# Two buffers for each block of parts, and a latents stage written out

## The reference

```python
xn = _layernorm(x)                               # mean and variance of a token's 256 numbers
q  = (xn @ Wqa @ Wqb).reshape(b, s, 16, 16)      # by way of 64 numbers a token
kv = (xn @ Wkva @ Wkvb).reshape(b, s, 4, 16, 2)  # by way of 32
k, v = kv[..., 0], kv[..., 1]
q, k = _rope(q), _rope(k)                        # pairs of numbers, turned by cos and sin of the position
logits = xn @ Wg                                 # the experts' router, 8 numbers a token
```

## Time and profile before

| | |
|---|---|
| median of 3 runs | 2279.63 us (2269.03 to 2282.21) |
| the profiled execution | 2277.82 us |
| its span, first to last instruction | 2275.8 us |
| TensorE busy | 2041.2 us, 90% |
| VectorE busy | 1575.5 us, 69% |
| ScalarE busy | 984.8 us, 43% |
| POOL busy | 514.2 us, 23% |
| mean granted TensorE clock over the span | 0.918 |

### The profile page before, as it was taken

The page is one execution under the profiler, slowest core; times in us unless marked ns, Lnnn a source line. Parts: engine busy times, 40 slices in busy tenths (PEclk is TensorE's granted clock), DMA queues, the critical chain, the costliest instruction groups (busy, mean ns, idle before and its releaser), DMA issues. The chain is left out here.

```text
span 2275.8 us, 36321 instructions
## 1 busy us (share of the span) xinstructions
PE 2041.2 (90%) x11618; PEld 1224.9 (54%) x11650; DVE 1575.5 (69%) x3508; ACT 984.8 (43%) x2128; POOL 514.2 (23%) x944
## 2 busy tenths in 40 slices
PE   7869999999999999999499999957728999999998
PEld 3322333333333333332399999945515777777777
DVE  5659998888888888882333333327737899999993
ACT  2222667777777677778344544411111111111112
POOL 2450123322222222222233333346500000000000
PEclk9656999999999999999799999976658999999998
DMA  4445001111111111100522232125430000000005
GB/s 137 141 166 188 27 22 65 58 46 42 43 42 43 41 43 44 41 12 11 158 84 89 89 103 95 52 65 154 146 119 22 19 19 19 19 19 10 10 10 162
DMA packets 124881, 152.22 MB, mean 67 GB/s; under 512 B 12952, under 2 KB 111904, under 8 KB 123808
## 3 DMA queue, kind: packets, MB, share of 16 engines
q1 hardware_dynamic: 85584, 99.48, 13.5%
q10 hardware_dynamic: 31440, 29.62, 3.9%
q0 software_dynamic: 7680, 20.98, 2.9%
HBM read 89.29 MB, written 60.29 MB: 66 GB/s over the span
## 5 line engine op out<-in xcount | busy, mean ns | idle before, releaser
L703 ACT ACTIVATE at_wt<-at_B 128x512 f32<-128x512 f32 (+3 forms) x1280 | 606.1, 538 | 251.1 <-PE at_B L753 244.3
L954 DVE TENSOR_REDUCE at_piece_max<-at_A 128x1 f32<-128x512 f32 x768 | 487.3, 683 | 52.7 <-PE at_A L734 50.8
L771 PE MATMUL at_O<-at_wt,at_v 128*32 128x512 f32 (+3 forms) x2560 | 312.3, 540 | 0.0
L657 POOL TENSOR_SCALAR_AFFINE_SELECT at_wt<-at_wt 128x128 f32<-128x128 f32 x512 | 148.0, 294 | 667.1 <-ACT at_wt L703 658.5
L734 PE MATMUL at_A<-at_k,at_q 96*128 96x512 bf16 (+3 forms) x800 | 275.3, 353 | 8.5 <-DVE at_piece_max L951 2.4
L951 DVE CUSTOM_DVE_ANT_0 at_junk<-at_A,at_hide 128x128 bf16<-128x128 f32 (+3 forms) x512 | 230.7, 487 | 73.0 <-PE at_A L734 69.1
L753 PE MATMUL at_B<-at_q,at_k 99*128 99x512 bf16 (+3 forms) x800 | 273.1, 349 | 5.2 <-ACT at_wt L703 5.2
L1392 PE MATMUL ex_H<-ex_xT,ex_w_in 128*128 128x256 f32 x1920 | 247.7, 285 | 3.2 <-DVE ex_xT L1499 3.2
L1392 PEld LDWEIGHTS ex_H<-ex_xT,ex_w_in 128*128 128x128 f32 x1920 | 236.8, 193 | 3.6 <-DVE ex_w_out L1504 3.6
L1513 DVE TENSOR_TENSOR ex_h<-ex_act_a,ex_H 128x256 f32<-128x256 f32 x160 | 67.2, 420 | 226.8 <-ACT ex_act_a L1441 226.7
L734 PE MATMUL at_A<-s_k,s_q 96*128 96x512 bf16 (+2 forms) x480 | 175.8, 384 | 21.5 <-PEq L93 10.6
(11 more groups left out here) (251 smaller groups left out, 2739.0 us busy)
## 6 DMA issues: line engine op xcount, KB each, us to landing
buf<-s_down ACTq DMA_DIRECT2D x10, 1024.0 KB, 11.0
ex_x<-buf SPq DMA_DIRECT2D x40, 256.0 KB, 2.7
expert_out<-ex_y ACTq DMA_DIRECT2D x40, 256.0 KB, 2.1
ex_raw_in<-in_W_in SPq DMA_DIRECT2D x8, 1024.0 KB, 5.0
q_parts<-parts SPq DMA_DIRECT2D x16, 384.0 KB, 4.8
x<-in_x SPq DMA_DIRECT2D x8, 512.0 KB, 4.5
xn<-xn SPq DMA_DIRECT2D x8, 512.0 KB, 5.3
at_v<-v SPq DMA_DIRECT2D x16, 256.0 KB, 3.5
```

Source lines behind the costliest of these rows:

```text
L657: pool.affine_select(block_, block_, [[1, P]], ALU.is_ge, 0.0, base=0, channel_multiplier=-1).then_inc(hidden, 1)
L703: act.activation(wt[(HP * p + h) % NE_][:, q0:CH], pB_of(p, h, u)[:, q0:CH], ACT.Exp, scale=D ** -0.5).then_inc(wt_ready, 1)
L771: pe.matmul(pO[j % 2][rows, q0:CH], vs[n % 3][:, kt // TPC, kt % TPC, :], wt[(HP * p + h) % NE_][:, q0:CH], start=kt < 2 and not late, sto ...
L954: ins = dve.tensor_reduce(top, pA[slot % NA][:, 0:w], AX.X, ALU.max)
```

## The change

Only `latents` is changed. It does four things.

```diff
-        x = [sb(f"x{u}", [P, TPC, E]) for u in range(2)]
+        x = [s["down"][:, u * TPC:(u + 1) * TPC] for u in range(2)]
...
-        parts = [sb(f"parts{k}", [P, PARTS, CH], BF16) for k in range(3)]
+        parts = [[sb(f"parts{k}{u}", [P, PARTS, CH], BF16) for u in range(2)] for k in range(3)]
...
-        def rounds(eng, chunk):
-
-            with eng.Fori(0, ROUNDS - 2) as j:
-                for u in range(2):
-                    chunk(2 * j + u, u, 4)
-            for c in range(NCH - 4, NCH):
-                chunk(c, c % 2, NCH - 1 - c)
+        def wait(eng, sm, v):
+
+            if v > 0:
+                eng.wait_ge(sm, v)
...
+            def parts_store(c, k):
+                sp.wait_ge(low_ready, PAIRS * c + k + 1)
+                dst = d["q_parts"][:, k * P:(k + 1) * P] if k < 2 else d["k_parts"]
+                sp.dma_start(dst[:, :, c * CH:(c + 1) * CH].rearrange("a p n -> p a n"),
+                             parts[k][c % 2][0:rows_of(k)]).then_inc(parts_out[c % 2], 16)
...
             for c in range(2):
-                xn_store(c, c, True)
-            rounds(sp, chunk)
+                xn_store(c)
+            for c in range(NCH):
+                parts_store(c, 0)
+                v_store(c)
+                if c + 2 < NCH:
+                    xn_store(c + 2)
+                for k in range(1, PAIRS):
+                    parts_store(c, k)
+                if NQ <= c < NCH - 1:
+                    first_heads(c - NQ)
...
             def turned(c, k):
 
-                pool.wait_ge(pair_used, 2 * (PAIRS * c + k) + 6)
+                pool.wait_ge(pair_used, 2 * (PAIRS * c + k) + 2)
+                wait(pool, high_ready, PAIRS * (c - 1) + k + 1)
...
-            def chunk(c, u, behind):
+            for c in range(NCH):
                 turned(c, 0)
-                for k in range(1, PAIRS):
-                    turned(c, k)
-                    left(c, k - 1)
-                left(c, PAIRS - 1)
-
-            rounds(pool, chunk)
+                left(c, 0)
+                turned(c, 1)
+                turned(c, 2)
+                left(c, 1)
+                left(c, 2)
...
             def high(c, k):
                 act.wait_ge(rot_ready, PAIRS * c + k + 1)
-                act.wait_ge(parts_out[k], 16 * (c + 1))
-                act.copy(parts[k][0:rows_of(k), 0], rot[k][0:rows_of(k)]).then_inc(high_ready, 1)
+                wait(act, parts_out[c % 2], 16 * PAIRS * (c // 2))
+                act.copy(parts[k][c % 2][0:rows_of(k), 0], rot[k][0:rows_of(k)]).then_inc(high_ready, 1)
...
-            def chunk(c, u, behind):
+            def chunk(c):
+                if c + 1 < NCH:
+                    xnT_copy(c + 1)
                 high(c, 0)
-                if behind:
-                    xnT_copy(c + 1, 1 - u)
+                mid(c, 0)
                 high(c, 1)
-                mid(c, 0)
-                if behind:
-                    comb_copy(c + 1, 1 - u)
+                if c + 1 < NCH:
+                    comb_copy(c + 1)
                 high(c, 2)
+                if c + 2 < NCH:
+                    std_of(c + 2)
                 mid(c, 1)
-                if behind >= 2:
-                    std_of(c + 2)
-                mid(c, PAIRS - 1)
+                mid(c, 2)
...
-            rounds(pe, chunk)
+            for c in range(NCH):
+                pe.wait_ge(comb_ready, c + 1)
+                pair(c, 0)
+                if c + 1 < NCH:
+                    turn(c + 1)
+                pair(c, 1)
+                pair(c, 2)
+                if c + 1 < NCH:
+                    combined(c + 1)
+                v_and_logits(c)
...
+            def chunk(c):
+                ahead = c + 2 < NCH
+                products(c, 0)
                 if ahead:
-                    statistics(c + 2, u, c // 2 + 2)
-                low(c, 0)
+                    statistics(c + 2)
+                products(c, 1)
+                products(c, 2)
                 if ahead:
                     variances(c + 2)
+                low(c, 0)
+                values(c)
+                if ahead:
+                    normalise(c + 2)
                 low(c, 1)
-                if ahead:
-                    normalise(c + 2, u, c // 2 + 2)
                 low(c, 2)
```

More of the change, by code:

```diff
@@ L197, in _, with xn_store @@
-            for k in range(PAIRS):
-                sp.sem_inc(parts_out[k], 16)
-            def xn_store(c, u, load):
-                sp.wait_ge(xn_ready, 4 * c + 4)
-                if load:
-                    sp.dma_start(x[u][:], one(x_rows, c + 2)).then_inc(x_in[u], 16)
-                sp.dma_start(one(xn_rows, c), xn[u][:]).then_inc(xn_out[u], 16)
-            def chunk(c, u, behind):
-                if behind >= 2:
-                    xn_store(c + 2, u, behind == 4)
-                sp.wait_ge(vl_ready, 2 * c + 4)
-                sp.dma_start(d["v"][bass.ds(c, 1)].rearrange("o h p n -> p (o h) n"),
-                             vtok[u][:].rearrange("p h t n -> p h (t n)")).then_inc(v_out[u], 16)
[L212 to L218, removed]
+            def xn_store(c):
+                u = c % 2
+                sp.wait_ge(xn_ready, 4 * c + 4)
+                if c + 2 < NCH:
+                    sp.dma_start(x[u], x_rows[c + 2]).then_inc(x_in[u], 16)
+                sp.dma_start(xn_rows[c], xn[u][:]).then_inc(xn_out[u], 16)
@@ L320, in _, with turn, combined, pair @@
             std_of(1)
-            xnT_copy(0, 0)
-            comb_copy(0, 0)
-            rounds(act, chunk)
+            xnT_copy(0)
+            comb_copy(0)
+            for c in range(NCH):
+                chunk(c)
         @block.tensor
         def _(pe):
-            def turn(c, u):
+            def turn(c):
                 pe.wait_ge(xn_ready, 4 * c + 4)
-                pe.wait_ge(xnT_ready, 2 * c + 2)
-                if not isinstance(c, int) or c:
-                    pe.wait_ge(vl_ready, 2 * c)
+                wait(pe, xnT_ready, 2 * c)
+                wait(pe, vl_ready, 2 * (c - 1))
                 for t in range(TPC):
                     for k in range(EC):
-                        ins = pe.transpose(pT[:, k, t * P:(t + 1) * P], xn[u][:, t, k * P:(k + 1) * P], ident[:])
+                        ins = pe.transpose(pT[:, k, t * P:(t + 1) * P], xn[c % 2][:, t, k * P:(k + 1) * P], ident[:])
                 ins.then_inc(xnT_made, 1)
-            def combined(c, u):
-                pe.wait_ge(xnT_ready, 2 * c + 4)
-                pe.wait_ge(comb_ready, c + 1)
+            def combined(c):
+                pe.wait_ge(xnT_ready, 2 * c + 2)
+                wait(pe, comb_ready, c)
                 for k in range(EC):
-                    ins = pe.matmul(pC[:], wcomb[:, k, :], xnT[u][:, k, :], start=(k == 0), stop=(k == EC - 1))
+                    ins = pe.matmul(pC[:], wcomb[:, k, :], xnT[c % 2][:, k, :], start=(k == 0), stop=(k == EC - 1))
                 ins.then_inc(comb_made, 1)
-            def pair(c, u, k):
-                n, m = PAIRS * c + k, (PAIRS * u + k) % 2
-                pe.wait_ge(pair_used, 2 * n + 2)
+            def pair(c, k):
+                n = PAIRS * c + k
+                wait(pe, pair_used, 2 * n - 2)
                 for a in range(2):
@@ L350, in pair, with v_and_logits @@
                     rows = slice(0, QL) if k < 2 else slice(QL, LAT)
[L351 removed]
+                    ins = pe.matmul(pR[n % 2][0:rows_of(k), a], w, comb[c % 2][rows, :], start=True, stop=True)
                 ins.then_inc(pair_made, 1)
[L354 to L355 removed]
+            def v_and_logits(c):
+                wait(pe, vl_ready, 2 * c)
                 for t in range(TPC):
[L357 removed]
+                    pe.matmul(pV[:, t, :], comb[c % 2][QL:LAT, t * P:(t + 1) * P], wv[QL:LAT, :], start=True, stop=True)
@@ L358, in v_and_logits @@
                 for t in range(TPC):
                     cols = slice(t * P, (t + 1) * P)
-                    ins = pe.transpose(pL[:, t, :], comb[u][LAT:COMB, cols], ident[LAT:COMB, LAT:COMB])
+                    ins = pe.transpose(pL[:, t, :], comb[c % 2][LAT:COMB, cols], ident[LAT:COMB, LAT:COMB])
                 ins.then_inc(vl_made, 1)
[L363 to L377, removed]
             pe.wait_ge(ident_in, 16)
-            turn(0, 0)
+            turn(0)
             pe.wait_ge(weights_in, 16 * 5)
-            combined(0, 0)
+            combined(0)
             pe.wait_ge(swapped, 6)
-            rounds(pe, chunk)
+            for c in range(NCH):
+                pe.wait_ge(comb_ready, c + 1)
[7 more added lines that the diff above has]
+                v_and_logits(c)
@@ L417, in low, with values @@
+                dve.tensor_tensor(by_sin[k][0:rows], pR[n % 2][0:rows, 1], sin[0:rows, at], ALU.mult).then_inc(pair_used, 1)
             def low(c, k):
                 dve.wait_ge(mid_ready, PAIRS * c + k + 1)
-                dve.tensor_tensor(parts[k][0:rows_of(k), 2], rest[k][0:rows_of(k)], parts[k][0:rows_of(k), 1],
```

(17 more changed lines are left out.)

71 lines of the change are left out of this document (33 added, 38 removed).

## The result

| | median, us | runs | |
|---|---|---|---|
| before | 2274.89 | 20 (2261.93 to 2286.04) | |
| after | 2289.18 | 20 (2277.88 to 2303.78) | ratio 1.0056, 95% interval 1.0036 to 1.0076 |

The change makes the kernel slower by 0.6%. The forecast was 0.7% faster, and its range ended at 2285. The profiled execution took 2286.24 us (span 2284.5), 8.4 more than that of before.

What follows compares the result with a forecast made beforehand. TensorE was taken to bound most latents chunks, waiting in others. Gains of 12.0 (waits), 1.0 (clock) and 2.2 (end) sum to 15.2 us, the stage going from 160.1 to 144.9: forecast 2263 us, range 2238 to 2285.

Steps and rivals of the forecast that it cites:

- Nothing after 160.1 us is touched, so all of the change is decided here: Stages behind latents: claimed to be untouched, so the whole effect would fall within the latents stage's 160.1 us.
- The `Fori` goes: ... so 0: Latents stage: removing the loop's register moves and branches, which cost TensorE nothing visible, would gain 0.
- rarer grants in the latents stage: Rival, TensorE in every chunk: the new order gets fewer 2.4 GHz grants, 5.6 us slower, 2283; chance 0.12.
- The 12.0 us of waits: Latents, TensorE: 10.5 us ahead of `combined` for `xnT_copy` and 1.5 us ahead of `turn` would go.
- `turn` has no wait: Latents, TensorE: `turn`, placed after `pair(c,0)`, would no longer wait for the logits copy; 1.5 us gained.
- The end: End of latents: `v` and two parts stored earlier, so `k_parts` lands sooner; 2.2 us gained, bounds 1 and 3.
- Sum of the stage: Whole latents stage: gains of 12.0 + 1.0 + 2.2 = 15.2 us, from 160.1 to 144.9.
- The clock: Latents, chunks 3 and 5: high clock time no longer idled away gains 1.0 us; about a fifth of work at 2.4 GHz.
- clock rival: Latents, TensorE: either 2.4 GHz is kept once granted, 2243 (chance 0.24), or grants become rarer, 2283 (0.12).
- The floor of 11.5 us a chunk: Latents, VectorE: its busy time of 11.4 and 11.2 us limits a chunk to about 11.5 us whatever TensorE's clock.
- VectorE against POOL: Latents, `low`s beside POOL: loss kept at 1.0 us a chunk; by the skill's exclusion rule 3.6, floor about 14 us.
- POOL 7.8 at most: Latents, POOL: its queue takes at most 7.8 us a chunk, shorter than VectorE's.

Runs made afterwards that it cites:

- e5: The changed kernel with ten already finished waits (five instructions) ahead of ScalarE's attention loop, which then begins at 447; ratio 0.9985 to the kernel before.
- e6: The kernel before with fourteen already finished waits (seven instructions) ahead of ScalarE's attention loop, moving it from 435 to 442; ratio 1.0098.
- e8: The kernel before with two buffers for each parts block and `x` in `s["down"]`, old orders and loop kept; ratio 0.9954.
- e9: The changed kernel with one buffer for each parts block again and ten finished waits ahead of ScalarE's attention loop; ratio 0.9972 to the kernel before.
- e1: The changed kernel with eight already finished waits (four instructions) ahead of ScalarE's attention loop, which then begins at 446; ratio 1.0089 to the kernel before.
- e3: The changed kernel with ScalarE's attention rounds written out, without the loop; ratio 0.9900 to the kernel before.
- e7: The changed kernel itself, run again in the second set; ratio 1.0032 to the kernel before.
- e4: The kernel before with ScalarE's attention rounds written out, without the loop; ratio 0.9937.

## Why the prediction was wrong

**The step that failed** stands at the start: "Nothing after 160.1 us is touched, so all of the change is decided here", and with it "The `Fori` goes: ... so 0". The text of attention is untouched; its place in ScalarE's instructions is not. Written-out chunks, other waits and no start values moved ScalarE's loop of attention from the 435th instruction to the 442nd, five short of an edge instead of twelve. There the wait for the instructions behind the edge was no longer covered by activations: attention took 21.7 us more in the profile. Idle instructions took the loss out of the changed kernel (e5) and put it into the kernel before (e6). None of the rivals had this place in it; the slower side was given to rarer grants in the latents stage, which did not come (30.7 us against 27.3).

- *The 12.0 us of waits.* Right in mechanism: TensorE's 10.5 us for `xnT_copy` became 1.6, in e8 2.2 and in e9 1.6. It was not seen that the new orders with one buffer would do.
- *`turn` has no wait.* Wrong: 3.9 us behind `normalise`. The prediction weighed `turn` against the logits copy and not against `normalise`, which moved too.
- *The end.* 3.2 us without an engine instead of 5.4, as said (2.2).
- *Sum of the stage.* 144.9 forecast, 147.9 measured; the new wait is of about that size.
- *The clock.* 30.7 us at 2.4 GHz in the stage instead of 27.3, about a fifth as forecast. Neither clock rival came true there. In e1's and e3's profiles it was 13.7 us and the stage took 158 to 159, so the grants in this stage vary by more than the change.
- *The floor of 11.5 us a chunk.* Too high: chunk 1 took 10.3 us with VectorE busy for 9.6. *VectorE against POOL* did not cost the 3.6 us a chunk that the prediction gave to the other case: the longest `low` took 1222 ns, where the kernel before had one of 2072. The 128-row `low`s average less than the 1194 ns of the earlier trace rows:

```profile
L412 DVE TENSOR_TENSOR parts<-rest,parts 128x512 bf16<-128x512 f32 x16 | 12.1, 757 | 3.1 <-ACT parts L279 3.1
```

- *POOL 7.8 at most* misreads, which have 8.12 and 8.05 in the last two chunks. Nothing hung on it.

What stays open: e5 was expected at 0.995 and measured at 0.9985. In the two profiles e5's attention is 19.8 us shorter than e7's, but its stages behind attention take 1182.9 us and e7's 1175.6, and the medians are 9.6 us apart. Over all profiles these stages took 1175.5 to 1183.6, the four with the bare stall 1175.5, 1175.6, 1177.7 and 1180.5; why is not known. Why an edge lies at the 447th instruction and how far the next ones lie was not measured.

## What to carry to other kernels

A change upstream moves every later instruction of its engine, so compare the profiles stage by stage, untouched stages first. Where a long loop sits on an engine that others wait for, time its rounds with and without the branch. A gap that stands ahead of the same instruction of the program, and ends the same time behind the branch, is a sign of instruction supply here, whatever releaser the profile names. What it costs depends on the work that lies between the loop's start and the edge. Write such a loop out, or shift it by a few idle instructions, before judging any other change by the total.

## What the runs showed of the hardware

A branch back over a body of 499 instructions cost ScalarE 2.4 to 3.0 us each time; in the kernels before and after, the loops of the shorter stages cost 0.1 to 0.3. The instruction at the edge started 4.4 to 5.1 us behind the branch wherever the loop began ahead of it. Seen from the one ahead of it, that is a stall of 2.1 to 2.3 us with 1 instruction ahead of the edge, 1.8 to 2.1 with 5, and 0.9 to 1.1 with 9, half of it covered by an activation; with the loop's start at the edge there was none.

The traces hold the transfers of instructions, of 8192 bytes each. In all nine profiled kernels with the loop one starts 0.9 to 1.2 us behind each of the six branches and another at 3.0 to 3.6; a third, at 5.1 to 5.7, is there only in the seven whose loop begins ahead of the edge. So the pieces come some 2.1 us apart, and ScalarE's first instruction and the one at the edge are 2.0 to 2.3 us apart too. (A few others lie between them, at different times in each branch.) The transfers come at the same times with the stall bare or covered; a count of them, such as this one for 6 us around the changed kernel's first branch, is 3 in e6, which has the stall, and does not tell it:

```profile
q14 instruction: 4, 0.03, 1.8%
```

The Trainium skill, page Runtime: NRT & Kernel Launch, section Instruction fetch mechanics, says that instructions come in blocks ahead of the sequencer, and that a taken branch to a block not held forces a fetch before execution goes on; the runs agree, and add that the block behind the target's is not there yet either. It says that kernels prefer full unrolling where possible, which e3 and e4 bear out (0.6 to 1.6%).
